# Eighteen row gathers per tile issued without a bounds check, with a zero row for the empty places

## The chip, the cores and the metric

The kernel runs on one NeuronCore of one Trainium2 chip. The metric is the time of one execution on the device in microseconds; the number quoted is the median of the runs.

## The reference, cut to what matters

A graph of 6250 nodes with 768 features each (float32) and 106250 directed edges (`src`, `dst`, sorted by `dst`, self loops included) goes through two graph convolutions and a soft mixture of experts. The change lies in the convolutions:

```python
def gcn_conv(x, edge_index, W, b, n_nodes):       # called twice, W1/b1 with a relu behind it, then W2/b2
    ...
    norm = dinv[src] * dinv[dst]
    h = x @ W.T
    msg = h[src] * norm[:, None]
    out = jax.ops.segment_sum(msg, dst, num_segments=n_nodes)
    return out + b
```

For every node the rows of its incoming neighbours are fetched, summed and multiplied by a 768x768 matrix. A node has 17 incoming edges on average, and the number differs from node to node.

## The kernel before, in words

The kernel keeps the scaled node rows in a table in HBM, one per layer: 6272 rows for the padded nodes, and behind them 128 rows of zeros (`ZERO_ROW` = 6272, `ROWS` = 6400). `zero_row` is a column of 128 numbers, 6272 + p for partition p. Nodes are handled in 49 tiles of 128, one node per partition.

For each tile 18 indirect DMAs (gathers) fetch 128 rows of 3072 bytes each from the table into `rows`. They come in two kinds:

- **13 "own" gathers.** Gather c brings for each node its c-th incoming row. A node with fewer edges names its zero row there, so that adding it does no harm. VectorE adds them one after the other (line 1116), a copy on ScalarE (line 786) starts the sum, and a plain load of the node's own row (`self_row`, line 509) is the last addend.
- **5 "left" gathers.** Edges past the 13th of any node of the tile are packed densely, in order, into 5 x 128 = 640 places. Gather c brings places 128c to 128c+127. TensorE multiplies each of the five 128-row blocks by a matrix of zeros and ones, `hot`, which sends every place to its node (lines 1378 to 1388); a place that is empty has a zero row in `hot` and counts for nothing. Since places are filled from the front, the empty ones are the last, almost all in left gather 4.

The row numbers are in `row_idx` and are copied to `gidx` by ScalarE one tile ahead (line 763). For left places VectorE works them out in layer 1, two tiles ahead, in six small steps (`pick_left`, lines 1002 to 1026): step 4 (line 1020) makes an addend of FAR = 16384 where the place is empty and of 0 elsewhere, and step 5 (line 1025) adds it to the picked row number. An empty place then names a row outside the table. Layer 2 uses the same `row_idx`.

Every gather is issued by GpSimd (`step`, lines 653 to 682) with `bounds_check=bound` and `oob_is_err=False`: an index over 6399 moves no row. The own gathers have the same check, though none of their indices lies outside.

The order of issue within a tile is fixed by `RUNS`: own 0, left 0, own 1 to 3, left 1, own 4 and 5, left 2, own 6 to 8, left 3, own 9 and 10, left 4, own 11 and 12. There is one buffer per gather. So ahead of an own gather GpSimd waits until VectorE has added the row of the tile before (`added`), and ahead of left gather r until TensorE has summed left block r of the tile before (`left_summed`, line 1388).

TensorE's order in a tile t: left block 0, six transposes of the finished aggregate of tile t-1 (line 1336), left blocks 1 to 4, the matrix product of tile t-1 (`dense`, line 1360, 24 matmul records). In layer 1 it waits ahead of `dense` for `left_ready`, the end of VectorE's step 5 (line 1405), and places the search for left edges (`find_left`, line 1302) behind it; VectorE's step 0 (line 1006) waits for that search. In layer 2 there are instead, between left blocks 3 and 4, six transposes of an output tile (line 1347, which wait for ScalarE's copy of line 816), and behind `dense` the router scores (line 1372). ScalarE's copy of the transposed aggregate (line 816) has to stand ahead of `dense`.

The gathers share the 16 DMA engines with the loads and stores that SyncE issues (`self_row`, line 509; stores, line 530; in layer 2 also loads of x, line 540).

The tail of the kernel, experts and output, uses no gather.

Of the kernel before, what the change touches and what calls it, by code (L numbers as in the profile page):

```python
# [53 lines left out]
FAR = 16384.0  # L54
# [3 lines left out]
def build(nc, a):  # L58
# [6 lines left out]
    ALU = mybir.AluOpType  # L65
# [3 lines left out]
    with ctx:  # L69
        def sb(name, shape, dt=f32):  # L70
            return ctx.enter_context(nc.sbuf_tensor(name, shape, dt))
# [4 lines left out]
        def sem(name):  # L76
            return ctx.enter_context(nc.semaphore(name))
# [37 lines left out]
        gidx = sb("gidx", [P, 2, CHUNKS], i32)  # L115
# [4 lines left out]
        zero_row = sb("zero_row", [P, 1])  # L120
# [4 lines left out]
        pick_col = sb("pick_col", [P, 3, PICKS])  # L125
# [26 lines left out]
        found = work[:, :, H:H + PICKS // 2 * COLS].rearrange("p h (c n) -> p h c n", c=PICKS // 2)  # L152
# [4 lines left out]
        def groups(ap):  # L157

            return ap.rearrange("p (h c) -> p h c", h=2)
# [61 lines left out]
        rows_in = [sem(f"rows_in{c}") for c in range(CHUNKS)]  # L221
# [93 lines left out]
        def over_pool(pool, l, bound, nth, nth16, tile, tile16):  # L315

            def chunk(t, i):
                pool.wait_ge(O["idx_ready"], nth)
                pool.sem_inc(O["wait_taken"], 1)
                if l == 0:  # L320
                    pool.wait_ge(s["zeros_out"], 32)
                for b in range(X_LANES if l == 0 else 2):
                    pool.wait_ge(*((y_out[b], y_count(b)) if l == 0 else (L[0]["stored"][b], done_count(b, 2))))
                pool.indirect_dma_start(over_rows, None, table[l][0:ROWS, :],
                                        bass.IndirectOffsetOnAxis(ap=over_idx[:, 0:1], axis=0),
                                        bounds_check=bound, oob_is_err=False).then_inc(O["rows_in"], 16)
                pool.reg_add(nth, nth, 1)
            over_loops(pool, chunk)
# [264 lines left out]
        def _(pool):  # L593
# [41 lines left out]
            for (t0, t1), landed in zip(WINDOW_PARTS, windows_in):  # L635
                for t in range(t0, t1):
                    pool.indirect_dma_start(windows_i[:, t, :], None, src_windows[:, :],  # L637
                                            bass.IndirectOffsetOnAxis(ap=anchor[:, t:t + 1], axis=0),
                                            bounds_check=last_anchor, oob_is_err=False).then_inc(landed, 16)
            pool.wait_ge(s["starts_ready"], 1)  # L640
            bound = pool.to_reg(ROWS - 1)
# [3 lines left out]
            for l in range(2):  # L645
                S = L[l]

                def counters():
                    pool.reg_mov(idx_needed, PEELED + 1)
                    pool.reg_mov(added_needed, OWN * (PEELED - 1) + 1)  # L650
                    pool.reg_mov(summed_needed, LEFT * (PEELED - 1) + 1)

                def step(i, k):
                    t = 2 * i + k
                    known = isinstance(i, int)
                    if known and t >= T:
                        return
                    pool.wait_ge(S["idx_ready"], t + 1 if known else idx_needed)
                    if not known:
                        pool.reg_add(idx_needed, idx_needed, 1)  # L660
                    def gather(slot):
                        pool.indirect_dma_start(  # L662
                            rows[:, slot, :], None, table[l][0:ROWS, :],
                            bass.IndirectOffsetOnAxis(ap=gidx[:, k % 2, slot:slot + 1], axis=0),
                            bounds_check=bound, oob_is_err=False).then_inc(rows_in[slot], 16)

                    for r, run in enumerate(RUNS):
                        if not known:
                            pool.wait_ge(S["added"], added_needed)
                            pool.reg_add(added_needed, added_needed, RUNS[r + 1][-1] - max(run[-1], 1)  # L670
                                         if r + 1 < len(RUNS) else OWN + 1 - run[-1])
                        elif t >= 1:
                            pool.wait_ge(S["added"], OWN * (t - 1) + max(run[-1], 1))
                        for c in run:
                            gather(SLOT["own", c])
                        if r < LEFT:
                            if not known:
                                pool.wait_ge(S["left_summed"], summed_needed)
                                pool.reg_add(summed_needed, summed_needed, 1)
                            elif t >= 1:  # L680
                                pool.wait_ge(S["left_summed"], LEFT * (t - 1) + r + 1)
                            gather(SLOT["left", r])
                over_pool(pool, l, bound, *counts)
                layer_sweep(pool, step, counters)
# [200 lines left out]
        def _(dve):  # L885
# [116 lines left out]
            def pick_left(t, n):  # L1002
                c = L[0]["pick_step"]
                if n == 0:
                    dve.wait_ge(L[0]["left_found"], t + 1)
                    dve.tensor_tensor(groups(pick_col[:, 0, :]), groups(slot_of[:, :]), found[:, :, :, 1],  # L1006
                                      ALU.subtract).then_inc(c, 1)
                elif n == 1:
                    dve.wait_ge(c, 5 * t + 1)
                    dve.tensor_tensor(pick[:, :, :], pick_iota.unsqueeze(1).to_broadcast([P, PICKS, EXTRA]),  # L1010
                                      pick_col[:, 0, :].unsqueeze(2).to_broadcast([P, PICKS, EXTRA]),
                                      ALU.is_equal).then_inc(c, 1)
                elif n == 2:
                    dve.wait_ge(c, 5 * t + 2)
                    dve.tensor_tensor(pick_halves, pick_halves, found[:, :, :, 2:COLS], ALU.mult).then_inc(c, 1)
                elif n == 3:
                    dve.wait_ge(c, 5 * t + 3)
                    dve.tensor_reduce(pick_col[:, 1, :], pick[:, :, :], AX.X, ALU.add).then_inc(c, 1)
                elif n == 4:
                    dve.tensor_scalar(groups(pick_col[:, 2, :]), found[:, :, :, 0], 0.0, FAR, ALU.is_equal, ALU.mult  # L1020
                                      ).then_inc(c, 1)
                elif n == 5:
                    dve.tensor_copy(left_node[:, ds(t, 1), :].rearrange("p t (h c) -> p (t h) c", h=2), found[:, :, :, 0])
                    dve.wait_ge(c, 5 * t + 5)
                    dve.tensor_tensor(row_idx[:, ds(t, 1), 0:LEFT], pick_col[:, 1, 0:LEFT].unsqueeze(1),  # L1025
                                      pick_col[:, 2, 0:LEFT].unsqueeze(1), ALU.add).then_inc(L[0]["left_ready"], 1)
# [484 lines left out]
```

## Time and profile before

| | |
|---|---|
| median of 3 runs | 3055.51 us (3054.37 to 3058.86) |
| the profiled execution | 3031.99 us, span 3030.3 us |
| GpSimd busy | 1838.2 us (61%) |
| VectorE busy | 1812.2 us (60%) |
| TensorE matmuls busy | 2157.9 us (71%) |
| the 1764 layer gathers on GpSimd | 1760.1 us, 998 ns each |
| HBM read and written | 826.10 MB and 82.00 MB |

"Busy" is the time in which an engine worked on an instruction; waits and the issue of DMAs by SyncE and ScalarE are not in it. A gather's duration on GpSimd is the time in which its descriptors are made, not the transfer. "Granted clock" is the share of its full 2.4 GHz at which TensorE ran.

### The profile page before, as it was taken

Reading aid. Unit: us, or ns where it says so; the run is one execution under the profiler, and the core shown is the slowest. Engines: PE = TensorE matmul, PEld = TensorE weight load, DVE = VectorE, ACT = ScalarE, POOL = GpSimd, SP = SyncE. Lnnn points to the kernel's source line nnn. Section 1 sums busy time; section 2 is a strip of 40 time slices with the busy share of each in tenths; the row PEclk is TensorE's granted clock in tenths of the full one; section 3 lists DMA queues with packets and bytes.
Section 4 is the critical chain, followed back from the end, with each engine's and each line's share of the span. In section 5 each row is a group of like instructions: output and inputs, shape, how many; then the busy total and the mean of one; then the engine's idle time right before and its main releaser. Section 6 shows DMA issues by size and latency. Waiting matters only on the chain.

```text
span 3030.3 us, 27648 instructions
## 1 busy us (share of the span) xinstructions
PE 2157.9 (71%) x7718; PEld 1314.9 (43%) x7719; DVE 1812.2 (60%) x2352; ACT 531.4 (18%) x985; POOL 1838.2 (61%) x1853
## 2 busy tenths in 40 slices
PE   6616777767677767777656777777777777777768
PEld 6613444434344434444323444444444444444424
DVE  7646566666666656666546566666656666666416
ACT  7830101111101010111001111111111111111300
POOL 3247676666666767666566666666666666666100
PEclk9997888888888888888877888888988888888889
DMA  9488888888888888888678988888888888888648
GB/s 332 175 338 301 287 291 293 291 285 288 287 291 293 300 292 290 295 289 292 229 261 296 315 312 303 301 302 298 307 299 305 314 305 307 295 301 316 237 148 311
DMA packets 237825, 876.71 MB, mean 289 GB/s; under 512 B 63260, under 2 KB 64044, under 8 KB 237756
## 3 DMA queue, kind: packets, MB, share of 16 engines
q0 software_dynamic: 143808, 671.74, 64.3%
q1 hardware_dynamic: 66132, 162.17, 14.8%
q10 hardware_dynamic: 27836, 42.21, 3.8%
q8 instruction: 23, 0.38, 0.0%
q14 instruction: 26, 0.21, 0.0%
HBM read 826.10 MB, written 82.00 MB: 300 GB/s over the span
## 4 chain that ended last, share of the span: by engine, by line
issue 23%; DVE 21%; another core or an unknown queue 19%; DMA 13%; POOL 12%; PE 6%; ACT 3%; DVEq 1%; POOLq 0%; ACTq 0%; SPq 0%
DVE acc L1116 14%; POOL rows L662 11%; DMA rows<-table_layer,gidx 10%; PE work L1360 2%; ACT logits L727 1%; DVE work L1135 1%; ACT xsT L716 1%; DVE hot L1075 1%; DVE agg L1116 1%; PE left L1386 1%; DMA rows<-xnew 1%; DMA out_x<-xstage 1%; PE acc L1485 1%; PE left L1436 0%
## 5 line engine op out<-in xcount | busy, mean ns | idle before, releaser
L662 POOL DMA_INDIRECT rows<-table_layer,gidx x1764 | 1760.1, 998 | 795.6 <-issue 484.2
L1116 DVE TENSOR_TENSOR acc<-acc,rows 128x768 f32<-128x768 f32 x1176 | 1134.0, 964 | 403.6 <-DMA rows<-table_layer,gidx 199.8
L1360 PE MATMUL work<-WT,aggT 128*128 128x384 f32 x2352 | 893.4, 542 | 262.0 <-DVE row_idx L1025 175.0
L1386 PE MATMUL left<-rows,hot 128*128 128x384 f32 x1960 | 812.9, 550 | 186.9 <-issue 97.6
L1360 PEld LDWEIGHTS work<-WT,aggT 128*128 128x128 f32 x2352 | 504.2, 217 | 660.4 <-issue 219.9
L1386 PEld LDWEIGHTS left<-rows,hot 128*128 128x128 f32 x1960 | 383.9, 211 | 468.6 <-issue 188.7
L816 ACT ACTIVATE aggT<-fixed 128x768 f32<-128x768 f32 x98 | 79.4, 810 | 1642.2 <-remote 1554.5
L1347 PE MATMUL fixed<-ident,xs 128*128 128x128 f32 x294 | 70.8, 409 | 228.2 <-issue 208.1
L1006 DVE TENSOR_TENSOR pick_col<-slot_of,work 128x6 f32<-128x6 f32 x49 | 7.9, 161 | 280.0 <-remote 273.5
L1347 PEld LDWEIGHTS fixed<-ident,xs 128*128 128x128 f32 x294 | 53.4, 212 | 262.0 <-issue 239.0
L786 ACT ACTIVATE acc<-rows 128x768 f32<-128x768 f32 x98 | 79.8, 814 | 434.3 <-issue 312.6
L1121 DVE COPY logits<-work 128x32 f32 (+1 forms) x49 | 9.4, 191 | 243.1 <-remote 232.2
L1161 DVE TENSOR_TENSOR agg<-left,agg 128x768 f32<-128x768 f32 x98 | 93.9, 958 | 75.5 <-remote 40.6
L1116 DVE TENSOR_TENSOR agg<-acc,self_row 128x768 f32<-128x768 f32 x98 | 93.8, 957 | 16.8 <-remote 12.7
L1336 PE MATMUL fixed<-ident,agg 128*128 128x128 f32 x588 | 86.1, 281 | 18.6 <-issue 16.2
L1336 PEld LDWEIGHTS fixed<-ident,agg 128*128 128x128 f32 x588 | 73.4, 145 | 53.1 <-issue 37.7
L1279 PE MATMUL left<-rows 125*128 125x49 bf16 x850 | 79.2, 269 | 20.0 <-POOL steps_down L623 20.0
L1279 PEld LDWEIGHTS left<-rows 125*128 125x128 bf16 x850 | 78.4, 142 | 20.3 <-POOL steps_down L623 19.7
L1372 PEld LDWEIGHTS work<-sp_c,xsT 128*128 128x128 f32 x588 | 74.4, 195 | 16.8 <-ACT xsT L803 3.2
L1075 DVE TENSOR_TENSOR hot<-acc,left_node 128x640 f32<-128x640 f32 x98 | 79.9, 815 | 0.4 <-DVE xsT L1052 0.4
L1302 PEld LDWEIGHTS work<-xsT,before_end 128*128 128x128 f32 x490 | 67.1, 203 | 21.6 <-issue 9.6
L637 POOL DMA_INDIRECT rows<-src_windows,ynext x49 | 50.4, 1028 | 42.6 <-DVEq L940 28.0
(309 smaller groups left out, 1330.2 us busy)
## 6 DMA issues: line engine op xcount, KB each, us to landing
self_row<-table_layer SPq DMA_DIRECT2D x98, 384.0 KB
rows<-table_layer,gidx POOLq DMA_INDIRECT x1764
xstage<-in_x SPq DMA_DIRECT2D x67, 384.0 KB
xs<-in_x SPq DMA_DIRECT2D x58, 384.0 KB
xnew<-xs SPq DMA_DIRECT2D x49, 384.0 KB
table_layer<-ynext SPq DMA_DIRECT2D x48, 384.0 KB
table_layer<-xstage ACTq DMA_DIRECT2D x40, 384.0 KB
xstage<-xnew SPq DMA_DIRECT2D x21, 384.0 KB, 5.7
```

Source lines behind the costliest of these rows:

```text
L662: pool.indirect_dma_start(rows[:, slot, :], None, table[l][0:ROWS, :], bass.IndirectOffsetOnAxis(ap=gidx[:, k % 2, slot:slot + 1], axis=0) ...
L786: act.activation(acc[:, :, 0:H], halves(rows[:, SLOT["own", 0], :]), ACT.Copy).then_inc(S["first_copied"], 1)
L816: act.activation(halves(aggT[:, :, :].rearrange("p k n -> p (k n)")), turned[:, :, 0:H], ACT.Copy).then_inc(S["aggT_ready"], 1)
L1075: dve.tensor_tensor(hot[:, b, 0:LEFT, :], iota_ps.unsqueeze(1).to_broadcast([P, LEFT, P]), left_node[:, ds(t, 1), 0:LEFT].rearrange("p t c ...
L1116: dve.tensor_tensor(acc[:, :, 0:H] if n < OWN - 1 else halves(agg[:, :]), acc[:, :, 0:H], halves(row), ALU.add).then_inc(S["added"], 1)
L1161: dve.tensor_tensor(halves(agg[:, :]), left[:, :, 0:H], halves(agg[:, :]), ALU.add).then_inc(S["agg_ready"], 1)
L1279: m = pe.matmul(mm[:, 0, 0:T], oh_low[:, g % 2, :, j], oh_high[:, g % 2, :, j], start=(g == 0 and j == 0), stop=(g == GROUPS - 1 and j == ...
L1336: m = pe.transpose(turned[:, kc // 3, (kc % 3) * P:(kc % 3 + 1) * P], agg[:, kc * P:(kc + 1) * P], ident[:, :])
L1347: m = pe.transpose(turned[:, kc // 3, (kc % 3) * P:(kc % 3 + 1) * P], xs[:, side, kc * P:(kc + 1) * P], ident[:, :])
L1360: m = pe.matmul(work[:, h, 0:H], aggT[:, kc, :], WT[l][:, kc, h * H:(h + 1) * H], start=kc == 0, stop=kc == KC - 1)
L1372: m = pe.matmul(work[:, 1, H:H + SLOTS], xsT[:, 0, kc, :], sp_c[:, kc, :], start=kc == 0, stop=kc == KC - 1)
L1386: m = pe.matmul(left[:, h, 0:H], hot[:, b, c, :], rows[:, slot, h * H:(h + 1) * H], start=c == 0, stop=c == LEFT - 1)
```

## The change

The gathers lose the two arguments of the check, and VectorE's step 4 multiplies by the partition's zero row number in place of FAR. An empty left place then names row 6272 + p, a row of zeros in the table, which is fetched like any other. The check's register and the checks of two other kinds of gathers (lines 324 and 637) stay.

```diff
@@ -661,8 +661,8 @@
                     def gather(slot):
                         pool.indirect_dma_start(
                             rows[:, slot, :], None, table[l][0:ROWS, :],
-                            bass.IndirectOffsetOnAxis(ap=gidx[:, k % 2, slot:slot + 1], axis=0),
-                            bounds_check=bound, oob_is_err=False).then_inc(rows_in[slot], 16)
+                            bass.IndirectOffsetOnAxis(ap=gidx[:, k % 2, slot:slot + 1], axis=0)
+                            ).then_inc(rows_in[slot], 16)
@@ -1017,7 +1017,7 @@
                 elif n == 4:
-                    dve.tensor_scalar(groups(pick_col[:, 2, :]), found[:, :, :, 0], 0.0, FAR, ALU.is_equal, ALU.mult
+                    dve.tensor_scalar(groups(pick_col[:, 2, :]), found[:, :, :, 0], 0.0, zero_row[:, 0:1], ALU.is_equal, ALU.mult
                                       ).then_inc(c, 1)
```

## Rows read from the trace of the kernel before

**Rows 1.** The page: span, busy time by engine, and the DMA queue of GpSimd

```profile
span 3030.3 us, 27648 instructions
PE 2157.9 (71%) x7718; PEld 1314.9 (43%) x7719; DVE 1812.2 (60%) x2352; ACT 531.4 (18%) x985; POOL 1838.2 (61%) x1853
q0 software_dynamic: 143808, 671.74, 64.3%
```

**Rows 2.** Timeline of GpSimd over one tile of layer 1 (start us, us)

```profile
770.16 1.00 POOL L662 DMA_INDIRECT rows<-table_layer,gidx  x1 [3.15 <-remote]
771.46 0.99 POOL L662 DMA_INDIRECT rows<-table_layer,gidx  x1 [0.30 <-issue]
...
788.39 1.01 POOL L662 DMA_INDIRECT rows<-table_layer,gidx  x1 [0.31 <-issue]
...
796.45 1.00 POOL L662 DMA_INDIRECT rows<-table_layer,gidx  x1 [3.14 <-remote]
```

**Rows 3.** Timeline of TensorE over the same tile of layer 1

```profile
787.36 4.04 PE L1386 MATMUL left<-rows,hot 128*128 128x384 f32 x12
792.82 1.56 PE L1386 MATMUL left<-rows,hot 128*128 128x384 f32 x4 [1.43 <-DMA rows<-table_layer,gidx]
```

**Rows 4.** Timeline of GpSimd over one tile of layer 2

```profile
2241.07 1.00 POOL L662 DMA_INDIRECT rows<-table_layer,gidx  x1 [3.20 <-remote]
...
2255.39 0.99 POOL L662 DMA_INDIRECT rows<-table_layer,gidx  x1 [0.30 <-issue]
...
2267.38 1.00 POOL L662 DMA_INDIRECT rows<-table_layer,gidx  x1 [3.18 <-remote]
```

**Rows 5.** Timeline of TensorE over the same tile of layer 2

```profile
2242.60 2.77 PE L1386 MATMUL left<-rows,hot 128*128 128x384 f32 x4
2260.62 1.46 PE L1386 MATMUL left<-rows,hot 128*128 128x384 f32 x3 [0.72 <-DMA rows<-table_layer,gidx]
```

**Rows 6.** Waits of layer 1, 240 to 1480 us (us in total, times, longest)

```profile
PE left L1386 <- issue: 35.9, 41, 3.8
PE left L1386 <- DMA rows<-table_layer,gidx: 28.7, 24, 3.6
```

**Rows 7.** Waits of layer 2, 1545 to 2800 us

```profile
PE left L1386 <- DMA rows<-table_layer,gidx: 52.5, 37, 2.5
PE left L1386 <- issue: 46.9, 35, 6.7
```

**Rows 8.** Sources: min/median/max ns of GpSimd's layer gathers, window gathers and plain loads

```profile
L662 POOL DMA_INDIRECT rows<-table_layer,gidx x1764: 992/998/1257, 222.9 to 2812.6; - x196
L637 POOL DMA_INDIRECT rows<-src_windows,ynext x49: 992/997/1278, 125.0 to 189.0; - x49
L630 POOL DMA_DIRECT2D ynext<-in_W x12: 536/538/736, 20.2 to 96.4; - x12
```

**Rows 9.** Engine windows (width, busy by engine, clock, DMA share, GB/s): layers, then short stretches

```profile
240.00:1480.00 1240.00, 897.51 (x2821) 522.89 (x2822) 768.64 (x1134) 124.54 (x187) 856.20 (x858) 0.85 0.85 291
1545.00:2800.00 1255.00, 928.96 (x3149) 565.25 (x3148) 771.64 (x852) 214.37 (x417) 857.27 (x860) 0.86 0.87 305
789.00:793.00 4.00, 2.57 (x9) 1.29 (x8) 0.00 (x0) 0.00 (x0) 3.09 (x4) 1.00 0.81 267
793.00:797.00 4.00, 1.38 (x4) 0.50 (x4) 2.07 (x5) 0.81 (x1) 0.86 (x2) 0.93 0.59 204
2150.00:2154.00 4.00, 4.00 (x18) 2.51 (x16) 2.54 (x3) 0.00 (x0) 2.99 (x3) 1.00 1.01 406
```

**Rows 10.** Sources of VectorE's steps 4 and 0 (min/median/max ns)

```profile
L1020 DVE TENSOR_SCALAR pick_col<-work x49: 150/158/164, 165.0 to 1448.3; 128x6 f32<-128x6 f32 x49
L1006 DVE TENSOR_TENSOR pick_col<-slot_of,work x49: 154/161/163, 163.8 to 1443.1; 128x6 f32<-128x6 f32 x49
```

## The prediction

> **What bounds the kernel now.** I read the page first, then the timeline of one tile in each layer, then the waits over each layer. The page shows no engine near its span: TensorE 71%, GpSimd 61%, VectorE 60% [rows 1]. So the end is set by a chain that changes engines, and the timelines show it.
>
> In layer 1 GpSimd issues left gather 0 at 770.16, then one gather every 1.30 us, left gather 4 (14 places later) at 788.39, and left gather 0 of the next tile at 796.45 after a wait of 3.14 [rows 2]. The tile takes 26.29 us. TensorE summed left blocks 1 to 3 and then stood 1.43 us for a DMA until 792.82, that is, until left gather 4 had landed, 4.43 us after its issue [rows 3]. The release of the buffers (3.63 us later) lets GpSimd go on. So the loop is: 14 gathers (18.23), landing (4.43), sum and release (3.63). In layer 2 the same loop closes over left gather 3, 11 places after left gather 0: issued at 2255.39, landed 2260.62, next left gather 0 at 2267.38, tile 26.31 us [rows 4, 5]. There left block 4 is summed after the transposes and is never late.
>
> How often does the loop bind? In layer 1 TensorE's left sums wait 24 times for a DMA and 41 times for what the profile names no source, 28.7 and 35.9 us together [rows 6]; in layer 2 52.5 and 46.9 us [rows 7]. The stretches hold about 47.7 and 47.8 tiles (858 and 860 gathers [rows 9], 18 a tile): 1.35 us a tile in layer 1, 2.08 in layer 2. The rest of the time another loop sets the pace (TensorE's block of work and, in layer 1, VectorE's six steps). The gathers are therefore critical, but by no more than 64.6 + 99.4 = 164 us in all.
>
> **The change, part by part.**
>
> *The check, on 1764 gathers.* No gather without a check stands in the trace, so its price is bounded from both sides. From above: GpSimd's plain load of the same 128 rows of 3072 bytes takes 538 ns, a gather 998 [rows 8]; all that makes a gather indirect is 460 ns, and the check is at most that. From below: nothing. I exclude an added cost, since nothing takes the check's place. Between the ends I take nothing, by two rows: the layer gathers' minimum and median are 992 and 998 ns although the left ones hold many refused indices and the own ones none, and the window gathers, which fetch rows of another size from another table, take 992 and 997 [rows 8]. The duration depends on nothing in the indices. Work that never varies looks like a fixed sequence, in which a comparison is a small part or is made anyway. It is an inference, and the weakest one here.
>
> On the rule: the Trainium skill, "DMA: Bandwidth & Descriptors", section "Anatomy of one DMA", calls descriptor generation small, and the fixed cost of a DMA mostly the receipt of its last byte. For this kernel the trace disagrees: generation is 998 of every 1302 ns on GpSimd and paces the loop. By the page, a cheaper generation would be worth nothing, and its fit (2.0 us plus bytes/436e3) would put left gather 4 some 0.65 us later for the 0.284 MB added below; the sum would be +16 us, not +10.
>
> *The rows now fetched.* 1764 gathers of 128 x 3072 bytes are 693.6 MB; 12 weight loads of the same size and 49 gathers of 128 x 192 bytes add 4.7 and 1.2, so GpSimd's queue would carry 699.5 MB if no row were refused. It carried 671.74 [rows 1]. 27.8 MB, or 0.284 MB a tile (92 rows), were refused, and are fetched from now on. They are the last of the 640 places, so nearly all belong to left gather 4, which grows from some 36 rows to 128. The queue took 64.3% of 16 engines' 3030.3 us for its 671.74 MB, 2.90 us per MB [rows 1], so the added bytes are 0.82 us of all 16 engines per tile. Left gather 4 lands later by between 0 (the engines had room) and 0.82 us. Around its landing the engines are 0.81 and then 0.59 busy, and up to 1.01 at another time [rows 9]; they have some room, so I take half, 0.41.
>
> In layer 1 that falls on the loop where left gather 4 is waited for: 24 x 0.41 = 10 us; elsewhere VectorE's loop covers it. If that cover were gone in every tile and the full 0.82 counted, it would be 49 x 0.82 = 40 us. In layer 2 I cost it at nothing: left block 4 is summed only behind the transposes, in the tile shown at 2242.60, though its gather is issued three places after left gather 3 and the next tile's left 0 only after that again [rows 4, 5]; two own gathers behind it may land a little later, and a wait of over 3 us on GpSimd, in which the queue drains, follows each tile. If that drain were not enough, layer 2 would pay as in the third rival.
>
> *VectorE's step 4* reads a column where it had a constant, 49 times. It takes 158 ns, and step 0, of the same shape with two tensor operands, 161 [rows 10]. I cost it at nothing; the ends are 0 and 49 x 0.01 us. The own gathers' indices, TensorE's instructions and the semaphores stay the same.
>
> Sum: 3031.99 + 10 = 3042 for the profiled execution. The median of the runs shown, 3055.51, lies 23.5 above it; the same addend gives 3065.
>
> **The rivals.**
>
> *The check costs GpSimd time (faster).* It acts at the 1.30 us between gathers: a saving of d per gather brings left gather 3 forward by 11d and left gather 4 by 14d. The break-even lies at d = 10 / (11 x 49 + 14 x 24) = 0.011 us, about 1% of a gather; above that the change wins. For it: the margin is tiny, the loop is critical, 460 ns of indirection have to be spent on something. Against it: the constant durations [rows 8]. At d = 0.1 us layer 2 gains 1.1 x 49 = 54 us and layer 1 24 x (1.4 - 0.41) = 24 us: 3055.5 - 78 = 2978. At d = 0.16 it is 86 + 34, 2935. From about d = 0.19 in layer 2 (2.08/11) the other loops bind and the gain stops near 164 us: 2891.
>
> *Nothing that can be measured.* The check is free and the zero rows land in time: the engines have room for all of them, or d is about 0.01. Time 3055. For it: left gather 4 gates only half the tiles of layer 1. A measurement of this kernel can tell about 0.2%, 6 us, from no change.
>
> *The DMA engines become the bound (much slower).* They stand at 0.85 and 0.87 of their time over the layers, and at 1.01 and 406 GB/s in a stretch of layer 2 [rows 9]. If every added 0.82 us lengthened every tile, it would be 98 x 0.82 = 80 us: 3135. Against it: GpSimd's pause of 3 us, in which the engines fall to 0.59 [rows 9]. It decides from the point where the engines no longer drain in that pause. The Trainium skill ("DMA: Bandwidth & Descriptors", "Where 436 GB/s comes from") has loads from HBM bound at about 358 GB/s; the 406 of the stretch is above that, so the trace doesn't bear that ceiling out.
>
> *The change doesn't do what it says*: the unchecked gather could be built as the same instruction with a limit that is never reached. Then GpSimd's row stays as it is and the time is the forecast's; it is part of it.
>
> **How the numbers follow.** A free check: 0.58, of which the forecast (about +10, its own range 3055 to 3095) has 0.40, nothing measurable 0.14, the bound engines 0.04. The costly check has 0.42: 0.04 of it with a d so near 0.011 that nothing is seen, 0.38 faster. "Slower" is then 0.44 less the 0.02 in which the added time stays under 6 us: 0.42; "same" 0.14 + 0.04 + 0.02 = 0.20; "faster" 0.38. For the range, 0.1 of the chance lies above a saving of 0.16 us per gather and 0.04 beyond +40 us: 2935 to 3095. Cases of both signs are in it, and its upper part, 3055 to 3095, is the likeliest one's.
>
> **What would show it.** Right: layer gathers still at 998 ns and 1.30 us apart; GpSimd's queue at 699.5 MB; in layer 1 more and longer waits of the left sums for a DMA, a tile of about 26.5 us; layer 2's tile at 26.3. Wrong: a gather's median well under 998 ns, with a longer wait of GpSimd ahead of left gather 0 and shorter waits of left blocks 3 and 4 for a DMA; or a layer 2 tile longer by 0.8 us with the engines near 0.9 busy.

## The result, and the profile after

The changed kernel takes 3105.97 us (median of 4 runs, 3104.82 to 3108.35); beside it the kernel before takes 3054.94 (3050.82 to 3058.86). The ratio is 1.0173, 95% interval 1.0154 to 1.0192: **slower by 51 us** (1.7%). The forecast was 3065, its range 2935 to 3095. The direction is the forecast's, the size is not, and the way it comes about is neither the forecast's nor any rival's.

The page of the changed kernel, with the lines that answer to [rows 1] and [rows 8]:

```profile
span 3103.7 us, 27648 instructions
PE 2203.0 (71%) x7718; PEld 1341.4 (43%) x7719; DVE 1806.9 (58%) x2352; ACT 531.0 (17%) x985; POOL 1749.2 (56%) x1853
q0 software_dynamic: 143808, 699.67, 63.1%
L662 POOL DMA_INDIRECT rows<-table_layer,gidx x1764 | 1671.0, 947 | 953.3 <-issue 476.3
```

The span is 73.4 us longer, though GpSimd has 89 us less to do: a gather takes 947 ns where it took 998, and follows the one before after 1.25 us where it was 1.30. The check is not free; it costs 51 ns. (The trace of the kernel before is of an execution of 3031.99 us, 23 under its timed median, while the trace of the change is at its own; so the two traces lie 73 us apart and the medians 51.) The queue carries 699.67 MB, as worked out (699.5).

The timeline of GpSimd over a tile of layer 2, which answers to [rows 4]:

```profile
2227.14 0.95 POOL L662 DMA_INDIRECT rows<-table_layer,gidx  x1 [0.30 <-issue]
2232.52 0.94 POOL L662 DMA_INDIRECT rows<-table_layer,gidx  x1 [4.43 <-remote]
2233.77 0.95 POOL L662 DMA_INDIRECT rows<-table_layer,gidx  x1 [0.30 <-issue]
...
2253.80 0.95 POOL L662 DMA_INDIRECT rows<-table_layer,gidx  x1 [0.30 <-issue]
2258.84 0.94 POOL L662 DMA_INDIRECT rows<-table_layer,gidx  x1 [4.10 <-remote]
```

Eighteen gathers run without a break, then GpSimd stands for 4.43 and 4.10 us, where it stood 3.2 before. From the starts of all gathers over 40 tiles a layer: in layer 1 a tile took 26.17 us, of which GpSimd stood 2.72; now 26.60, with 4.07. In layer 2 it took 26.37 with 2.93; now 27.47 with 4.93. Eighteen gathers give 18 x 0.051 = 0.92 us a tile; the stand takes back 1.35 and 2.00. The balance, 0.43 and 1.10 us a tile on 49 tiles each, is 75 us: the 73.4 of the two spans. Some 22 of them are the fast execution that the trace of before caught.

What is the stand for? The waits of GpSimd in layer 2 (in total, times, longest):

```profile
POOL rows L662 <- PE left L1386: 195.1, 50, 6.4
POOL rows L662 <- remote: 39.2, 17, 7.3
```

It waits for TensorE's left sums, ahead of left gather 0 and hardly anywhere else; where the profile can't place the releaser it says "remote", and it is the same wait at the same gather. TensorE does not wait for rows in turn. Its waits in layer 1, and below them those in layer 2, against [rows 6] and [rows 7]:

```profile
PE fixed L1336 <- issue: 148.8, 93, 2.6
PE left L1386 <- issue: 130.1, 101, 11.9
PE left L1386 <- DMA rows<-table_layer,gidx: 3.2, 1, 3.2
```

```profile
PE left L1386 <- issue: 166.2, 120, 4.1
PE work L1372 <- issue: 122.9, 69, 2.7
PE left L1386 <- DMA rows<-table_layer,gidx: 14.7, 7, 4.0
```

The waits for a DMA have gone from 28.7 and 52.5 us to 3.2 and 14.7, and the kernel is slower all the same. What has grown is "issue", time before a matmul for which the profile names no source. It was there before, at other instructions; these were TensorE's longest waits before, in layer 1 and in layer 2:

```profile
PE work L1360 <- DVE row_idx L1025: 175.0, 31, 8.7
```

```profile
PE fixed L1347 <- issue: 200.3, 41, 9.4
```

In layer 1 the wait for VectorE's step 5 has fallen from 175.0 to 17.1 us, and all "issue" together has risen from 126 to 315; in layer 2 "issue" has risen from 253 to 323. TensorE's timeline over the same tile shows its form:

```profile
2238.90 7.90 PE L1360 MATMUL work<-WT,aggT 128*128 128x384 f32 x24
2246.64 1.42 PE L1372 MATMUL work<-sp_c,xsT 128*128 128x32 f32 x12
2247.90 1.54 PE L1386 MATMUL left<-rows,hot 128*128 128x384 f32 x4
2249.27 0.27 PE L1336 MATMUL fixed<-ident,agg 128*128 128x128 f32 x1
2250.76 0.27 PE L1336 MATMUL fixed<-ident,agg 128*128 128x128 f32 x1 [1.21 <-issue]
2252.89 0.27 PE L1336 MATMUL fixed<-ident,agg 128*128 128x128 f32 x1 [1.86 <-issue]
2255.68 0.37 PE L1336 MATMUL fixed<-ident,agg 128*128 128x128 f32 x1 [2.53 <-issue]
...
2257.82 4.35 PE L1386 MATMUL left<-rows,hot 128*128 128x384 f32 x7 [0.26 <-issue]
```

The product was sent off by 2246.6, the six transposes behind it trickle, and the semaphore that says "product done" is raised only at 2257.88 by the trace's semaphore events; the left sums' follow from there, and GpSimd goes on at 2258.84. **TensorE's signals come late.** From the start of the product's last matmul to the next signal recorded for it the median was 5.1 us (layer 1) and 5.4 (layer 2) before, and is 11.9 and 11.7 now. In the tail, where no gathers run, the like takes 0.50 us. Two cautions go with these medians. The trace of before holds only 38 and 42 of the 49 signals of a layer; by those alone that fall in their own tile the medians before are 2.7 and 4.8. And not every signal comes later now: in layer 2 that of the six transposes came 10.4 us after its matmul before and comes 0.43 now, that of the scores 11.9 and 7.3. They come in bursts, and the place of the burst in TensorE's order has moved.

The clock, by the windows of the two layers, against [rows 9]:

```profile
240.00:1480.00 1240.00, 904.07 (x2755) 519.82 (x2754) 751.30 (x1120) 124.09 (x185) 797.86 (x843) 0.84 0.84 296
1545.00:2800.00 1255.00, 898.82 (x2985) 551.95 (x2984) 733.85 (x817) 201.56 (x395) 781.41 (x826) 0.81 0.83 302
```

In layer 2 the granted clock fell from 0.86 to 0.81: 1.2 GHz for 10.1 us of a tile instead of 6.8. The DMA engines are busy no more than before (0.84, 0.83).

### The profile page after: what moved, and what is told of

The parts are those of the page before. It is cut to its first block, busy times and chain, and to the rows that moved or that the text cites. A ratio compares the mean times of both kernels' runs of the same rounds, so it can differ in the third digit from the quotient of the medians.

```text
span 3103.7 us, 27648 instructions
## 1 busy us (share of the span) xinstructions
PE 2203.0 (71%) x7718; PEld 1341.4 (43%) x7719; DVE 1806.9 (58%) x2352; ACT 531.0 (17%) x985; POOL 1749.2 (56%) x1853
## 3 DMA queue, kind: packets, MB, share of 16 engines
q0 software_dynamic: 143808, 699.67, 63.1%
## 4 chain that ended last, share of the span: by engine, by line
PE 34%; issue 26%; another core or an unknown queue 15%; DVE 13%; DMA 5%; POOL 3%; ACT 3%; DVEq 1%; ACTq 0%; POOLq 0%; SPq 0%
PE left L1386 13%; PE work L1360 12%; DVE acc L1116 7%; POOL rows L662 3%; PE work L1372 2%; DMA rows<-table_layer,gidx 2%; PE fixed L1336 2%; ACT logits L727 1%; ACT xsT L716 1%; PE fixed L1347 1%; DVE agg L1116 1%; DVE hot L1075 1%; DMA rows<-xnew 1%; DMA out_x<-xstage 1%
## 5 line engine op out<-in xcount | busy, mean ns | idle before, releaser
L662 POOL DMA_INDIRECT rows<-table_layer,gidx x1764 | 1671.0, 947 | 953.3 <-issue 476.3
L1386 PE MATMUL left<-rows,hot 128*128 128x384 f32 x1960 | 919.2, 603 | 330.7 <-issue 309.7
L1360 PE MATMUL work<-WT,aggT 128*128 128x384 f32 x2352 | 803.2, 499 | 81.4 <-issue 39.5
L1386 PEld LDWEIGHTS left<-rows,hot 128*128 128x128 f32 x1960 | 444.2, 238 | 711.1 <-issue 571.1
L1360 PEld LDWEIGHTS work<-WT,aggT 128*128 128x128 f32 x2352 | 454.7, 195 | 420.8 <-issue 82.4
L1336 PE MATMUL fixed<-ident,agg 128*128 128x128 f32 x588 | 134.1, 345 | 193.9 <-issue 191.6
L1336 PEld LDWEIGHTS fixed<-ident,agg 128*128 128x128 f32 x588 | 98.3, 180 | 250.5 <-issue 240.4
L1372 PE MATMUL work<-sp_c,xsT 128*128 128x32 f32 x588 | 78.7, 265 | 128.6 <-issue 126.0
L1372 PEld LDWEIGHTS work<-sp_c,xsT 128*128 128x128 f32 x588 | 81.0, 200 | 114.1 <-issue 98.6
L803 ACT ACTIVATE xsT<-fixed 128x768 f32<-128x768 f32 x49 | 39.7, 811 | 215.0 <-issue 116.9
```

Source lines behind the costliest of these rows:

```text
L662: pool.indirect_dma_start(rows[:, slot, :], None, table[l][0:ROWS, :], bass.IndirectOffsetOnAxis(ap=gidx[:, k % 2, slot:slot + 1], axis=0) ...
L1336: m = pe.transpose(turned[:, kc // 3, (kc % 3) * P:(kc % 3 + 1) * P], agg[:, kc * P:(kc + 1) * P], ident[:, :])
L1360: m = pe.matmul(work[:, h, 0:H], aggT[:, kc, :], WT[l][:, kc, h * H:(h + 1) * H], start=kc == 0, stop=kc == KC - 1)
L1372: m = pe.matmul(work[:, 1, H:H + SLOTS], xsT[:, 0, kc, :], sp_c[:, kc, :], start=kc == 0, stop=kc == KC - 1)
L1386: m = pe.matmul(left[:, h, 0:H], hot[:, b, c, :], rows[:, slot, h * H:(h + 1) * H], start=c == 0, stop=c == LEFT - 1)
```

## The experiments

The kernels stand in five groups. Those of a group ran on one chip, with the kernel before beside them, and each result is read against that; the second and the fifth group ran on the same chip, and the third and the fourth on one more each. The chip of the first group was used for it alone, so whether its speed belongs to the chip or to the occasion is not shown; "chip" stands for both below.

### The parts of the change (first group)

e1 takes the check off the 13 own gathers alone, and keeps FAR; e2 has the zero row and all checks; e3 has the zero row and takes the check off the 5 left gathers.

```
 e1:  **(dict(bounds_check=bound, oob_is_err=False) if slot < LEFT else {})
 e2:  FAR -> zero_row[:, 0:1]          (line 1020 alone)
 e3:  as e2, and  ... if slot >= LEFT else {}
```

> The check is taken off the 13 own gathers alone; the left gathers keep it and their empty places still name a row outside, so no row more is fetched than before. Theory P (pace: faster gathers move the loop onto TensorE, which then runs longer at 1.2 GHz): 13 of 18 gathers take 947 ns, the time comes out over before by more than half of the 51 us that the change cost, 3080 to 3106, and layer 2's mean granted clock falls from 0.86 towards 0.81. Theory B (bytes: the 28 MB of zero rows cost it, the faster gathers by themselves gain): under before, 3000 to 3045, clock 0.86 or more.

> The zero rows alone: empty left places name a zero row, all gathers keep the check and its 998 ns. Theory P: near before, 3055 to 3070 (the +10 us of the prediction for a free check), granted clock 0.85 to 0.87, tile of layer 2 at 26.3 us. Theory B: near the change, 3095 to 3110, clock 0.84, tile of layer 2 at 27.4 us.

> Zero rows, and the check taken off the 5 left gathers alone. Five gathers of 947 ns move left gather 4 forward by only 0.2 to 0.25 us. Theory P: between the zero rows alone and the change, nearer to the former, 3060 to 3080. Theory B: at the change's time, 3095 to 3110.

Measured, against a kernel before that takes 2748.15 us here and not 3055, so that none of the expected times applies: e1 2684.69, ratio 0.9768 (0.9752 to 0.9784); e2 2748.35, 1.0004 (0.9994 to 1.0013); e3 2730.04, 0.9935 (0.9918 to 0.9952). **The zero rows cost nothing, and the missing check is a gain**, 51 ns at a time: 13 x 0.051 x 98 = 65 us, and e1 has 63 less. e3 has 18 less of 25. Here the same kernel ran 300 us faster than in the result. Windows of e1 over its layers:

```profile
240.00:1400.00 1160.00, 894.54 (x2934) 504.30 (x2934) 807.03 (x1173) 133.72 (x199) 863.73 (x896) 0.93 0.92 326
1450.00:2500.00 1050.00, 861.25 (x3151) 526.78 (x3149) 738.55 (x827) 213.55 (x416) 778.01 (x809) 0.95 0.95 349
```

and TensorE's timeline in layer 2 of e1:

```profile
2011.67 1.56 PE L1387 MATMUL left<-rows,hot 128*128 128x384 f32 x4 [1.52 <-DMA rows<-table_layer,gidx]
2015.53 1.56 PE L1387 MATMUL left<-rows,hot 128*128 128x384 f32 x4 [2.30 <-DMA rows<-table_layer,gidx]
2016.92 0.82 PE L1348 MATMUL fixed<-ident,xs 128*128 128x128 f32 x6
2018.75 1.56 PE L1387 MATMUL left<-rows,hot 128*128 128x384 f32 x4 [1.01 <-DMA rows<-table_layer,gidx]
```

TensorE waits for rows in every tile and, in layer 2, for hardly anything else (183.9 us; in layer 1 also 36.9 us for VectorE's step 5). Its signals follow their last matmul in 0.3 to 0.5 us (median), and GpSimd never stands: the tile is 18 intervals between gathers long, 23.44 us in e2 (18 x 1.302) and 22.8 in e1. Each nanosecond of a gather counts there.

### The same on a chip like that of the result (second group)

e4 is the change, e5 and e6 are e1 and e2 again; e7 is the change with three of the six feature blocks of the dense product left out, so its output is not the reference's.

```
+ if kc in (1, 2, 3): continue         (e7, in dense, line 1358)
```

> The change as it is, once more, beside the kernel before. In the first experiments the kernel before took 2748 us where it had taken 3055, and TensorE gave its semaphores 0.29 to 0.5 us after the start of a stretch's last matmul, where it had been 5 to 12 us late for the dense product in the traces of 3030 and 3104. Theory T (whether TensorE delivers late decides the sign): where the kernel before takes about 2750 us, GpSimd's 18 gathers are the tile (18 x 1.302 = 23.4 us), and the change gives 18 x 0.051 x 98 = 90 us back, less what the engines can't follow: 2665 to 2700. Where the kernel before takes about 3055 us, the change is slower again by about 50. Theory S (the sign is the change's own, and only the check on the own gathers gains): slower than before, or equal, in both.

> The check off the 13 own gathers alone, no row more fetched. Theory T: where before takes about 2750, 0.977 of it as measured; where it takes about 3055, the faster pace alone costs most of the change's 51 us: 3080 to 3106. Theory B (there the zero rows cost it): 3055 or less.

> The zero rows alone, all gathers checked. Theory T: equal to before within 0.3% in either state of TensorE, since left gather 4 alone is a little later. Theory B: where before takes about 3055, 3090 or more.

> The change with half of the dense product left out (three of its six blocks of 128 features, in both layers), so that TensorE has some 4 us less work a tile at full clock; gathers, semaphores and order are the same. Theory T: where TensorE delivers late, its work bounds the tile, and the time falls by 150 us or more, to where the gathers bind (2700 to 2850); where it is prompt, the gathers bind already and the time stays within 1% of the change's. Against T: where the change is slow, leaving out this work moves it by less than 30 us.

Measured, before 3049.77: e4 3090.32, 1.0137 (1.0099 to 1.0175); e5 3079.96, 1.0104 (1.0064 to 1.0145); e6 3049.92, 1.0000 (0.9983 to 1.0017); e7 3019.69, 0.9909 (0.9879 to 0.9938). So the zero rows are innocent here too. The same edit of 13 gathers that gave 2.3% on one chip costs 1.0% on the other: 30 of the 41 us that the change loses here are theirs, and the loss is the faster gathers'. Half the dense product gone brings 71 us, neither the 150 of theory T nor the under 30 that would speak against it: TensorE's load is part of it, not all. The windows of layer 2, e6 and then e4 (columns as in [rows 9]):

```profile
1570.00:2800.00 1230.00, 962.04 (x3108) 561.24 (x3107) 752.12 (x832) 209.15 (x407) 832.16 (x836) 0.84 0.88 312
```

```profile
1570.00:2800.00 1230.00, 889.89 (x2991) 551.53 (x2990) 726.25 (x805) 200.99 (x396) 765.35 (x810) 0.81 0.84 303
```

The clock is 0.84 with checked gathers and 0.81 without; GpSimd stands 3.1 us a tile in e6 and 4.95 in e4, and the tile is 26.58 and 27.46 us. In layer 1 both kernels have a tile of 26.25 us. On this chip the whole loss is layer 2's: 0.88 x 49 = 43 us. The product's signal is late in e6 already, 3.3 us in layer 1 and 10.0 in layer 2 (10.1 and 11.6 in e4), with checked gathers and the time of the kernel before.

### Bytes, or the pace of the gathers (third group)

f1 is the change with gathers of half a row (1536 bytes; the second half of `rows` is cleared once at the start, which the cut below leaves out, and the output is not the reference's). f2 and f3 are the kernel before with 5 and 9 short pauses of GpSimd a tile; f4 is the change.

```
 f1: - rows[:, slot, :], None, table[l][0:ROWS, :],
     + rows[:, slot, 0:H], None, table[l][0:ROWS, :].rearrange("r (h d) -> (r h) d", h=2),
 f2: + if slot in PACED:    # the left gathers; f3: every second slot
     +     pool.memset(pace[:, :], 0.0).then_inc(s["iotas"], 1)
     +     pool.wait_ge(s["iotas"], paced)
```

> The change with each gather fetching 1536 bytes per index instead of 3072 (the table is read as rows of 384 numbers; the other half of each buffer is cleared once), so that GpSimd's pace and TensorE's and VectorE's work stay and the gathers' bytes are halved. Where the kernel before takes about 3050 us, TensorE's semaphores came in one burst within about 1 us of the DMA engines running empty, in five traces. Theory D (gather traffic holds TensorE's signals back): they come within 1 us of the last matmul now, layer tiles fall to 18 x 1.251 = 22.5 us, and the time to 2580 to 2720. Theory H (TensorE itself is slowed, whatever the DMA engines do): signals stay 5 us or more late and the time over 2950. Where before takes about 2750 us both give 2580 to 2700.

> The kernel before with GpSimd slowed down: behind each of the five left gathers it clears a column of 128 numbers and waits for that, about 0.2 to 0.4 us each, so 1 to 2 us a tile. Theory D: where before takes about 3050 us, the engines run empty more often, TensorE's signals come through earlier, and the slower issue makes the kernel faster or costs nothing: 2950 to 3050. Theory H, and the plain view that issuing later can only cost: slower, 3060 to 3200. Where before takes about 2750 us the issue paces the tile, and it is slower by 100 to 200 us.

> The same with nine such pauses, 2 to 3.5 us a tile. Theory D: where before takes about 3050 us still no slower than 3050 unless the issue alone (23.4 us plus the pauses) is longer than the 26.3 us of a tile; H: slower than the five pauses by 100 us or more. Where before takes about 2750 us: slower by 200 to 350 us.

> The change as it is. Where before takes about 2750 us: 2665 to 2700, faster by 2 to 3%, since there GpSimd's 18 gathers are the tile and each takes 51 ns less. Where before takes about 3050 us: slower by 1.2 to 1.8% as in the two measurements so far. The rival (the zero rows' 28 MB take back what the pace gives where the gathers bind) expects 2720 to 2760 in the first case.

Measured, before 3048.18: f1 3100.92, 1.0171 (1.0150 to 1.0192); f2 3137.32, 1.0289; f3 3435.35, 1.1270; f4 3094.37, 1.0152 (1.0129 to 1.0175). f1, window of layer 2:

```profile
1570.00:2800.00 1230.00, 892.16 (x2965) 547.98 (x2965) 726.04 (x805) 198.85 (x391) 774.72 (x818) 0.82 0.58 176
```

With 176 GB/s in place of 304 and the engines 0.58 busy, the time, the stand (3.95 and 4.68 us a tile) and the clock are close to f4's (3.92, 4.86; 0.81 in layer 2). **Neither bytes nor busy DMA engines delay TensorE.** The number of packets fell by a fifth only (115584 on GpSimd's queue for 143808), so their number is not excluded. Of the expectations, theory D falls here and H holds. The paced kernels say something else. GpSimd's timeline in f2, and TensorE's left sums in layer 2:

```profile
2203.46 1.00 POOL L666 DMA_INDIRECT rows<-table_layer,gidx  x1 [0.30 <-issue]
2204.46 0.11 POOL L671 MEMSET pace<- 128x1 f32 x1
2205.53 1.00 POOL L666 DMA_INDIRECT rows<-table_layer,gidx  x1 [0.95 <-POOL pace L671]
```

```profile
L1395 PE MATMUL left<-rows,hot 128*128 128x384 f32 x880 | 427.6, 618 | 325.7 <-DMA rows<-table_layer,gidx 317.4 <-issue 3.3 <-DVE agg L1170 3.1
```

A pause moves the next gather by 0.77 us (2.07 between starts for 1.30), more than the 0.2 to 0.4 expected. 23.44 + 5 x 0.77 = 27.3, and the tile is 27.43: GpSimd's own time, hardly a stand left (0.08 to 0.16 us). And TensorE, on a chip where it had been late, now waits 317 us for rows in a stretch of 45 tiles, 7 us a tile, with 3.3 us of "issue". It needs only some 20 us for a tile's work there, and its signals are prompt, a median of 0.5 us after the product's last matmul. The times of f2 and f3 are theory H's, the prompt signals are D's. The run can't tell whether TensorE is prompt because the gathers come farther apart or because it has time to spare.

### TensorE relieved and loaded (fourth group)

g1 and g2 are the change and the kernel before, both with fifteen matmuls a layer-2 tile left out; g3 is the kernel before with the dense product computed twice; g4 is the change.

```
 g1, g2: + if 0 < kc < KC - 1: continue                  (dense)
         - for h in range(2):                            (left sums)
         + for h in range(2 if c in (0, LEFT - 1) else 1):
         - for kc in range(KC):   + for kc in (0, KC - 1):   (score)
 g3:     - for part in parts:     + for part in [*parts, *parts]:
```

> The change with fifteen matmuls a layer-2 tile left out (feature blocks 1 to 4 of the dense product, the second half of left-over blocks 1 to 3, blocks 1 to 4 of the score), so that its output is not the reference's. Theory R (where the kernel takes about 3050 us, the rate at which TensorE gets through its matmuls sets the tile, and a faster gather is worth nothing until TensorE is relieved): the tile falls to eighteen gathers of 1.251 us, 22.5 us, and the time under 2850 us, below the light version of the kernel before. Theory W (TensorE's signals come late by a fixed time, however little work is before them): the time stays over 3000 us. On a chip where TensorE is prompt (before near 2750 us) both give 2650 to 2700 us, and the run tells nothing apart.

> The kernel before with the same fifteen matmuls a tile left out (its output is not the reference's). Theory R: the tile falls to eighteen gathers of 1.302 us, 23.44 us, and the time to 2720 to 2850 us, some 90 us over the light version of the change (eighteen times 0.051 us, 98 tiles). Theory W: over 3000 us, as the kernel before.

> The kernel before with the dense product computed twice in a row in every tile (twelve more matmuls; the second pass starts the sums anew, so the output is the same). Theory R on a chip where before takes about 3050 us: the tile grows by twelve times 0.32 to 0.70 us, 3.8 to 8.4 us, and the time by 370 to 820 us. Theory W: by less than 100 us. On a chip where TensorE is prompt: the extra 3.8 us fit mostly into TensorE's idle time, and the time grows by under 150 us.

> The change, unaltered. On a chip where before takes about 3050 us: 3090 to 3106 us, a ratio of 1.013 to 1.019, as before. On a chip where before takes about 2750 us: GpSimd's pace sets the tile, eighteen times 0.051 us less over 98 tiles is 90 us, 2650 to 2690 us, a ratio of 0.963 to 0.979, and under the 2685 us of the version with thirteen unchecked gathers unless the reads of left-over blocks come last.

Measured, before 3033.58: g1 2988.56, 0.9851 (0.9831 to 0.9870); g2 2975.63, 0.9808 (0.9788 to 0.9828); g3 3294.82, 1.0860 (1.0811 to 1.0909); g4 3062.23, 1.0098 (1.0081 to 1.0115). **Both theories fell.** Theory R asked for under 2850 of g1 and at least 370 us more of g3 (it is 261); theory W asked for over 3000 us of g1 and g2, and for under 100 us more of g3. With a third of TensorE's work gone the change is still 13 us slower than the kernel before (g1, g2). Windows of layer 2, g1 and g3:

```profile
1570.00:2800.00 1230.00, 623.40 (x1806) 360.14 (x1806) 762.20 (x856) 221.08 (x430) 787.67 (x831) 0.70 0.87 314
```

```profile
1570.00:2800.00 1230.00, 1103.53 (x3601) 678.90 (x3599) 650.13 (x723) 174.05 (x344) 726.48 (x727) 0.90 0.75 263
```

The doubled product in g3's timeline:

```profile
2201.80 15.64 PE L1360 MATMUL work<-WT,aggT 128*128 128x384 f32 x48
```

Twelve more matmuls are 24 more records, 7.7 us, and not the 3.8 that the expectation began at. With the 20.3 us that f2 showed for a tile's work that is an estimate of 28.0 us, and g3's tiles take 27.6 us in layer 1 and 29.9 in layer 2, where TensorE is busy 0.90 of the time. By this estimate TensorE's work nearly fills g3's tile, and the kernel before had some 6 us of room.

The clock goes against the edit each time: 0.70 with a third of the work gone (0.82 in g4), 0.90 with the product doubled (0.87 in the trace of before). A TensorE with less to do stands longer and is granted 1.2 GHz for more of the tile. That may be one reason why the tile moved only to 25.9 and 26.1 us (g1); no run changed the clock alone.

### Breaks in the train of gathers (fifth group)

If it is neither TensorE's load nor a fixed delay, what ends a long silence (5 us and more) of its signals? By the semaphore events of layer 1 (240 to 1480 us), all 46 silences of the changed kernel end while GpSimd stands, though it stands 16% of the time, and they end 3.45 us after its last gather (10% and 90% points 3.25 and 3.52); in g3, with checked gathers, 44 of 45, and 2.42 us after it (2.33 to 2.49). In f2, where GpSimd hardly stands, it is 1 of 93, and the silences are half as long (9.1 us for 21.0). That looked as if breaks let the signals through. It left out that in the kernel before it is 23 of 75 and in e6 30 of 78, and that on the chip of the first group e1 has silences nearly as long as f2's (8.7 us) with prompt signals. h1 is the change with four pauses a tile, h2 with three, h3 the kernel before with three.

```
+ PACED = (0, 1, 12, 15)     (h1)      + PACED = (0, 10, 14)     (h2, h3)
  (and the pause of f2)
```

> The change with four short pauses of GpSimd a tile (0.77 us each, as the runs of the kernel before with pauses had them), after gathers 2, 6, 11 and 15 of the eighteen; its output is the reference's. Theory P (on the chips where the kernel takes about 3050 us, a long train of gathers without a break holds up TensorE's signals, which come through only once GpSimd has stood still for 2.4 to 3.5 us; short breaks let them through, and the faster the gathers, the longer the stand): TensorE's signals are prompt, GpSimd no longer stands for left-over sums, and the tile is 18 x 1.251 + 4 x 0.77 = 25.60 us, 1.83 us under the 27.43 us of the kernel before with five pauses (3137 us), so 98 x 1.83 less: 2958 us, faster than both kernels. Theory R (TensorE's own rate sets the tile): the pauses win nothing, 3050 to 3120 us. Where the kernel before takes about 2750 us the pauses only cost: some 2950 us.

> The change with three such pauses a tile, after gathers 2, 8 and 14, six gathers apart. Theory P, if breaks six gathers apart are enough: 22.52 + 3 x 0.77 = 24.83 us a tile, 2882 us. If they are too far apart, GpSimd's stands of 3 to 4 us come back, and the time is 2950 to 3080 us. Theory R: 3050 to 3120 us.

> The kernel before with the same three pauses. Theory P: 23.44 + 3 x 0.77 = 25.75 us a tile, 2973 us, faster than the kernel without pauses although GpSimd is given more to do; some 90 us over the change with three pauses. Theory R: 3050 to 3100 us.

Measured, before 3034.00: h1 3049.04, 1.0046 (1.0019 to 1.0073); h2 3070.19, 1.0119 (1.0064 to 1.0175); h3 3024.37, 0.9970 (0.9951 to 0.9990). The expected 2958, 2882 and 2973 are missed widely. **Theory P fell too:** h1 gains on the change, but the signals that were to be prompt are not (the product's has a median of 8.2 and 8.9 us in h1, 4.7 and 10.9 in h3), and 3070 lies in the range of theory R, 3049 at its edge. h2 also lies in the range given for breaks too far apart, though its stands are some 2 us and not 3 to 4. Layer 2 of h1, its window and GpSimd's waits:

```profile
1570.00:2800.00 1230.00, 936.24 (x3112) 557.42 (x3110) 753.28 (x835) 209.21 (x409) 814.03 (x1026) 0.86 0.91 314
```

```profile
POOL rows L666 <- POOL pace L671: 82.5, 89, 1.0
POOL rows L666 <- remote: 29.3, 16, 2.5
POOL rows L666 <- PE left L1395: 23.1, 12, 3.9
```

What the runs show is that pauses and stands are exchangeable. h3 adds 3 x 0.77 = 2.3 us of pauses to each tile of the kernel before; the stands shrink from 2.72 and 2.93 us to 0.45 and 0.68, and the tile stays as it was: 26.10 and 26.33. In h1 the stands shrink to 1 us and the tile of layer 2 falls from the change's 27.2 to 27.5 us to 26.5, with the clock back at 0.86. Slowing GpSimd down undoes two thirds of the change's loss (1.0137 on that chip in the second group, 1.0046 here; the change itself was not run again beside h1). With all of TensorE's work in it, and GpSimd's own time for a tile anywhere from 22.5 to 25.8 us, the tile takes 26.0 us or more on these chips; only above that, in f2 and f3, does GpSimd set it.

## Why the prediction was wrong

**The price of the check.** "Between the ends I take nothing" is the step that failed first. Between 0 and 460 ns it is 51 ns, over the 11 ns of the break-even. The constant 992 to 998 ns showed that the duration does not depend on the indices, as it still does not (947 ns with all rows in the table). It did not show that the check is free: a check made on every index can be as constant as none.

**The rows now fetched.** The bytes were right (699.5 for 699.67 MB). The term "24 x 0.41 = 10 us" measured as nothing: 1.0004 and 1.0000, each within 0.2% (e2, e6). The ends were 0 and 0.82 us a tile, and 0 is the value. Whether the rows land early enough or the engines have room was not told apart. With this the forecast's only addend goes. Its 3065 would have become 3055.

**The step to the time.** With d = 0.051 us, and the zero rows at nothing, the rival of the costly check gives 11 x 0.051 x 49 = 27 us in layer 2 and 24 x 14 x 0.051 = 17 in layer 1: 3011. It came out 51 us above the kernel before. So the reading of what bounds the kernel was wrong as well, on this chip. The loop "14 gathers, landing, sum and release" stood on TensorE's waits for a DMA, 28.7 and 52.5 us. They were real, and they went away, but behind them was another loop that was as long: TensorE's signals, raised up to 12 us after their matmuls. It was in the trace: in the tile of [rows 5] the last of the left sums was sent off at 2262.99, and its signal was raised at 2266.8, with those of the transposes and the scores in one burst. The "release" ("3.63 us later") and the waits that "the profile names no source" for are that. I added the unnamed waits to the loop of the gathers and got 164 us "in all", when they belonged to the loop that a faster gather did not shorten. And I read the left sums' waits alone: TensorE's longest waits, 175.0 us for VectorE's step 5 in layer 1 and 200.3 us without a named source in layer 2, stood at other instructions and were not priced. On the chip where TensorE is prompt, the rival of the costly check is right and even too small: there e1 has 63 us with 13 gathers, and the tile of 18 intervals says that all 18 count in both layers.

One sum of the forecast is also off by itself: at d = 0.16 its formula gives 24 x (14 x 0.16 - 0.41) = 44 us in layer 1 and not 34, so 2925 in place of 2935. The outcome does not hang on it.

**What the change does, as shown.** The zero rows: nothing. The gathers: 0.92 us a tile sooner. Where TensorE is prompt that is a gain (2.3% for 13 of them; the whole change was not run on such a chip). Where it is late, GpSimd stands longer instead, by more than it gained: that the faster gathers are the cause is shown by e5 against e6, and h1 supports it. Layer 2 pays most, 1.10 of 1.53 us by the first two traces, and all of it in e4 against e6. There 3.3 us more of each tile are at 1.2 GHz; if all of that were TensorE's critical work it would cost half, 1.65 us. That the clock is the link from the longer stand to the longer tile fits the windows of layer 2 (0.81 in after and e4, 0.84 in e6, 0.86 in h1), but no run changed the clock alone.

On the page weighed in the prediction: on the chip of the first group, generation (998 ns of each 1302, e2) set the tile outright. The Trainium skill, "DMA: Bandwidth & Descriptors", section "Anatomy of one DMA", calls that part small; I had drawn from it that a cheaper generation would be worth nothing, and e1 has 63 us. Its fit for added bytes, +16 us, is not borne out either: they cost nothing.

**What stays open.** Why TensorE raises its signals late on some chips: not the bytes (f1), not its load alone (g1, e7), not the check or the zero rows (before is late too), and not in the tail, where no gathers run. Gathers farther apart made it prompt in f2, but there TensorE also had time to spare; what the rate acts through is not known, and the number of packets was not tried alone. Nor is it shown why a longer stand follows a faster gather: each of the theories named beforehand, R, W, D, H and P, has a run against it. Nor was it tried whether fewer, larger gathers would be treated otherwise.

Of the signs named in the prediction, the first for "wrong" came true: a gather's median well under 998 ns, a longer wait of GpSimd ahead of left gather 0, and shorter waits of the left blocks for a DMA. It went with a loss, where the rival that it stood for was a gain. The longer tile of layer 2 appeared with the engines at 0.83, not near 0.9.

## What to carry to other kernels

A wait that names a DMA is worth its length only if nothing unnamed is as long behind it, so read all waits of the consumer and not those of one line: before a producer is made faster, look how late its consumer's signals are raised, not only what the consumer waits for. Time given to an engine that stands once a tile for somebody else is time to stand, and TensorE was granted a lower clock where it had less to do (g1, 0.70 for 0.82). Measure an edit on more than one chip where it sits on such a balance: thirteen unchecked gathers were worth 2.3% on one and cost 1.0% on another.

## What the runs showed that was not expected

- The same kernel, before, took 2748 us on one chip and 3034 to 3055 on the others. On the first TensorE's signals follow in 0.3 to 0.5 us; on the others the product's has, without pauses and with the whole work, a median of 3 to 12; DMA engines at 0.93 and 0.97 did no harm there, and 354 GB/s were moved (e2, layer 2).
- Five pauses a tile (f2) make TensorE prompt on a chip where it was late, three or four (h1, h3) do not, and neither does moving half of the bytes (f1).
- Adding 2.3 us of pauses to a tile of GpSimd's work cost nothing (h3 was 0.3% faster, 0.9951 to 0.9990; the kernel before itself took 3050 and 3034 us in the two groups of that chip).
- Leaving out a third of TensorE's matmuls won 1.9% (g2), and the granted clock over the whole run fell from 0.86 to 0.74.
